# A kernel of four layers: every second weight of a 16-entry table is picked out by GpSimd, where it had every fourth

## The reference

```
layer 1  attention, 16 heads of 128 over 1024 rows (no mask), float32
layer 2  silu(x @ tern(W_up)) * (x @ tern(W_gate)) @ tern(W_down), tern(W) = clip(round(W / mean|W|)) * mean|W|
layer 3  causal attention over a latent of 64, 16 heads

def _ghost_linear(x, idx, lut):            # layer 4
    w = lut[idx]                           # lut has 16 float32 entries
    return jnp.einsum('bsh,oh->bso', x, w)
gate = _ghost_linear(x, gate_idx, lut)     # gate_idx, up_idx: 688 x 256 int32, 0..15
up   = _ghost_linear(x, up_idx, lut)
h    = jax.nn.silu(gate) * up
return _ghost_linear(h, down_idx, lut)     # down_idx: 256 x 688
```

## Time and profile before

| what | value |
|---|---|
| time, median of 3 runs | 882.39 us (881.47 to 882.75) |
| time of the profiled execution | 882.52 us |
| its span (first to last instruction) | 880.7 us |
| busy: PE, DVE, ACT, POOL | 93%, 87%, 69%, 49% of the span |
| instructions | 13310 |

### The profile page before, as it was taken

The page is one execution under the profiler, slowest core; times in us unless marked ns, Lnnn a source line. Parts: engine busy times, 40 slices in busy tenths (PEclk is TensorE's granted clock), DMA queues, the critical chain, the costliest instruction groups (busy, mean ns, idle before and its releaser), DMA issues.

```text
span 880.7 us, 13310 instructions
## 1 busy us (share of the span) xinstructions
PE 815.8 (93%) x4386; PEld 474.4 (54%) x4386; DVE 770.5 (87%) x1726; ACT 604.2 (69%) x1044; POOL 430.1 (49%) x459
## 2 busy tenths in 40 slices
PE   7889989999999989998998999989988999998997
PEld 3445544455455445454445454567755566564687
DVE  4888999999999999999999999856789898986646
ACT  5777767776778676776766776765765777768632
POOL 3334454444454448678769776125333454544300
PEclk8999999999999999999999999999989999999999
DMA  3588859957788668776875676821000000000001
GB/s 105 123 180 157 151 113 173 194 113 153 166 166 155 127 130 151 148 143 117 161 149 111 124 142 130 155 79 46 1 1 1 1 1 1 1 1 2 1 1 49
DMA packets 276869, 86.32 MB, mean 98 GB/s; under 512 B 267584, under 2 KB 272448, under 8 KB 276416
## 3 DMA queue, kind: packets, MB, share of 16 engines
q1 hardware_dynamic: 275520, 80.05, 47.0%
q0 software_dynamic: 992, 5.34, 2.2%
q10 hardware_dynamic: 288, 0.07, 0.0%
HBM read 17.29 MB, written 1.05 MB: 21 GB/s over the span
## 4 chain that ended last, share of the span: by engine, by line
DVE 41%; PE 38%; issue 9%; ACT 6%; DMA 3%; POOL 2%; DVEq 0%; SPq 0%; ACTq 0%; POOLq 0%
DVE EP L1689 11%; DVE ps L1674 10%; PE ps L1012 6%; PE ps L1014 5%; PE ps L1013 5%; PE ps L1035 4%; DVE ptm L1790 4%; PE ps L1246 3%; PE ps L1050 3%; PE ps L1281 3%; PE ps L1267 3%; DMA ET<-EP 2%; DVE OL L1750 2%; DVE ps L1873 2%; DVE rinv L1684 1%
## 5 line engine op out<-in xcount | busy, mean ns | idle before, releaser
L1445 ACT ACTIVATE EP<-ps,rinv 128x1024 f16<-128x1024 f32 x128 | 142.5, 1113 | 47.5 <-DVE rinv L1684 45.4
L1435 ACT ACTIVATE ps<-ps,nmax 128x1024 f32<-128x1024 f32 x128 | 139.3, 1088 | 49.2 <-DVE nmax L1674 42.8
L1674 DVE CUSTOM_DVE_ANT_0 ps<-ps,zero,q_unit 128x1024 f32<-128x1024 f32 x128 | 163.6, 1278 | 1.6 <-PE ps L1014 1.6
L1689 DVE SCALAR_TENSOR_TENSOR EP<-ps,rinv,EP 128x1024 f16<-128x1024 f32 x128 | 163.4, 1277 | 0.8 <-ACT EP L1445 0.5
L2039 POOL TENSOR_TENSOR wgu<-wgu,ptm 128x688 f32<-128x688 f32 x60 | 99.1, 1651 | 45.3 <-DVE ptm L1790 43.4
L1012 PE MATMUL ps<-ET,VH 128*128 128x512 f16 x256 | 97.0, 379 | 9.5 <-DMA ET<-EP 5.0
L1012 PE MATMUL ps<-K,Q 128*128 128x512 f16 x256 | 97.5, 381 | 8.7 <-DVE KR L1654 4.5
L2039 POOL TENSOR_TENSOR wdn<-wdn,ptm 128x512 f32<-128x512 f32 x45 | 57.2, 1272 | 93.2 <-DVE ptm L1790 92.1
L1014 PE MATMUL ps<-K,QR 128*128 128x512 f16 x256 | 97.0, 379 | 0.0
L1013 PE MATMUL ps<-KR,Q 128*128 128x512 f16 x256 | 97.0, 379 | 0.0
L1014 PE MATMUL ps<-ET,VL 128*128 128x512 f16 x256 | 97.0, 379 | 0.0
(11 more groups left out here) (256 smaller groups left out, 2119.3 us busy)
## 6 DMA issues: line engine op xcount, KB each, us to landing
wqr<-in_wqk SPq DMA_DIRECT2D x16, 256.0 KB, 3.6
wgu<-in_tern POOLq DMA_DIRECT2D x3, 1024.0 KB, 6.6
wvr<-in_wv SPq DMA_DIRECT2D x8, 256.0 KB, 4.1
wor<-in_wo SPq DMA_DIRECT2D x16, 128.0 KB, 3.1
ET<-EP SPq DMA_TRANSPOSE x128, 4.3
X<-in_x SPq DMA_DIRECT2D x2, 512.0 KB, 5.7
prw<-in_down_idx POOLq DMA_DIRECT2D x2, 256.0 KB, 5.1
tern<-in_l_wuq_rep SPq DMA_DIRECT2D x1, 512.0 KB, 4.1
```

The lines of the kernel that those rows point to most:

```text
L1435: e.activation(bank, bank, ACT.Exp, bias=nmax[:, c:c + 1], scale=-1.0, accum_out=rsum[:, c:c + 1]).then_inc(exped.sem, 1)
L1445: e.mul(EP[:, n % NE_RING, 0, :], SB(u, j), rinv[:, c:c + 1]).then_inc(e_hi.sem, 1)
L1674: e.tensor_tensor_reduce(SB(u, j), SB(u, j), zero[:, :].broadcast_to([P, 1024]), UNIT(h), 3.0e38, ALU.add, ALU.min, nmax[:, c:c + 1]).then ...
L1689: e.scalar_tensor_tensor(out=EP[:, n % NE_RING, 1, :], in0=SB(u, j), scalar=rinv[:, c:c + 1], in1=EP[:, n % NE_RING, 0, :], op0=ALU.mult, ...
```

## The change

The rule that says which picks GpSimd does goes from `v % 4 == 3` to `v % 2 == 1`. In each table GpSimd now makes the picks v = 1, 3, 5, ... 15 (eight, where it had four), and DVE makes v = 2, 4, ... 14 and v = 0. Half 1 of `ptm` is now written and read by GpSimd alone, and half 0 is written by DVE and read by GpSimd. Since DVE no longer makes pick 1, the add of v = 1 waits for DVE's v = 0 by a wait of its own (`picked[t, 0]`). Nothing else moves: the list of steps is the same.

```diff
-                (picked_g if v % 4 == 3 else picked).mark(t, v)
+                (picked_g if v % 2 == 1 else picked).mark(t, v)
...
-                    if v % 4 == 3:
+                    if v % 2 == 1:
                         continue
...
-                        if v % 4 == 3:
+                        if v % 2 == 1:
                             w.wait_ge(*index_in[t % 2][t])
                             w.wait_ge(*lut_in[0])
                             w.each([SUMS[step]])
                             e.tensor_scalar(ptm[:, 1, 0:n], index_tile(t), float(v), lut[:, v:v + 1], ALU.is_equal,
                                             ALU.mult).then_inc(picked_g.sem, 1)
-                        w.wait_ge(*(picked_g if v % 4 == 3 else picked)[t, v])
+                        w.wait_ge(*(picked_g if v % 2 == 1 else picked)[t, v])
                         if v > 1:
                             w.wait_ge(*lut_added[t, v - 1])
+                        else:
+                            w.wait_ge(*picked[t, 0])
                         e.tensor_tensor(dst, dst, ptm[:, v % 2, 0:n], ALU.add).then_inc(lut_added.sem, 1)
```

## The result

The changed kernel is slower: 886.27 us (median of 4 runs, 884.84 to 886.55) against 881.93 us (880.85 to 882.75), a ratio of 1.0041 with an interval of 1.0025 to 1.0057, that is 3.6 us. (The ratios in this document are those on record. They are not the quotients of the medians, which can differ by 0.1%: here 1.0049, or 4.3 us.) The forecast was 877.8 us and a range of 872.5 to 885.0. What came is nearest to the first rival, GpSimd's lateness on the path, some 2 us larger than it was priced. But 2.9 of the 3.7 us between the two profiled spans stand in two falls of TensorE's granted clock, which no rival had.

The account below looks back on a forecast made before the run. DVE was taken to set the pace in the 688-column tables, with PE and DVE taking turns before. The sum was 882.5 - 2.1 (small tables) - 3.5 (large tables) + 1.0 (`wol` wait) = 877.9, forecast 877.8 us, range 872.5 to 885.0.

Parts of the forecast that it names:

- the first rival: Tables of 688 columns: GpSimd's lateness reaches the path at `out_proj` and table 6, 3.8 us; 884.1 us in all, chance 0.19.
- GpSimd's busy sum: From 330 to 550 us, sixteen added picks bring GpSimd to 209 of 220 us busy, 95%, without the joints.
- The walk through GpSimd's new order: From 403.42 us in layer 1, GpSimd's steps followed one by one: `wol` ready at 421.6 instead of 417.7, 3.9 us late.
- PE stands still 0.9 us: PE waits for `wol` in `out_proj`, three times in the 688-column tables: 2.7 us if nothing hides it, 1 us charged.
- the 1.1 us at table 6: DVE's v = 0 of table 6 waits once for GpSimd's last add of table 5, about 1.1 us.
- I take half of the 7.0: Layer 1's 688-column tables: a gain of 3.5 us (bounds 0 and 7), as GpSimd also waits for others.
- The relief: 28 picks leave DVE, 19.6 us of work: 5.9 in the 512-column tables, 13.7 in those of 688.
- The picks' share of the chain: Path share of DVE's pick time: 35% at 512 columns, worth 2.1 us; 69% at 688, worth 9.5.
- The 7.0 of scarce engines: Three stretches from 337 to 545 us: layer 1 shortens by at most the scarcest engine's spare, 1.6 + 3.2 + 2.2 us.
- The port: DVE and GpSimd picks disturbing each other: taken as nil, 4 us either side; as third rival 21 us, 899 us, chance 0.03.

Follow-up runs that it names:

- large tables alone: The kernel before with the new pick rule only in tables 3 to 6 (688 columns): 886.95 us, ratio 1.0039 to before.
- relief alone: The changed kernel with GpSimd's new picks cut to two columns, except the first of tables 0 and 3: 876.68 us, 0.9922 of before.
- own index tile: The changed kernel with the odd tables' indices in a separate tile, so table 6 need not wait for table 5's last add: 887.21 us, 1.0048 of before.
- either edit alone: The changed kernel with only a separate tile for the odd tables' indices (887.21 us), or only the second split of `wo` moved earlier (887.52 us).
- edits alone: The kernel before, old pick rule, with a separate tile for the odd tables' indices and the second `wo` split earlier: 884.92 us, 1.0019 of before.
- early `wol`: The changed kernel with the second split of `wo` ahead of the splits of `wqk`: 887.52 us, 1.0051 of before.
- both edits: The changed kernel with a separate tile for the odd tables' indices and the second `wo` split earlier: 882.96 us, 1.0 of before.

## Why the prediction was wrong, step by step

**GpSimd's busy sum: right.** 209 us of 220 forecast, 208.19 measured. Its idle time before the adds of the large tables, 45.3 us in the earlier trace rows, of which 43.4 for DVE's picks, fell to 6.7, of which 1.9 for them (under 15 forecast).

**The walk through GpSimd's new order: right.** From the end of `q_unit` I had `wol` ready 18.2 us later. This is the stretch that answers to the earlier trace rows:

```profile
402.10 2.60 POOL L2034 TENSOR_SCALAR ptm<-prw,lut 128x688 f32<-128x688 int32 x1
404.78 3.42 POOL L2041 TENSOR_TENSOR wgu<-wgu,ptm 128x688 f32<-128x688 f32 x2
...
412.71 1.15 POOL L1993 TENSOR_TENSOR wql<-wqr,wqh 128x512 f16<-128x512 f32 x1
...
415.55 2.58 POOL L2034 TENSOR_SCALAR ptm<-prw,lut 128x688 f32<-128x688 int32 x1
418.21 1.64 POOL L2041 TENSOR_TENSOR wgu<-wgu,ptm 128x688 f32<-128x688 f32 x1
419.82 0.72 POOL L2015 TENSOR_TENSOR wol<-wor,woh 128x256 fp32r<-128x256 f32 x1
```

`wol` ends at 420.54, 18.4 us behind the start of the pick at 402.10. PE's wait there is 0.92 us, as forecast.

**"PE stands still 0.9 us", three times, of which I charged 1 us: too small.** I put the walk against PE as it ran before. PE gains a lead from DVE's relief, and then it waits for the lead as well: 1.60, 0.92 and 1.93 us, 4.4 in all. The same error is in the 1.1 us at table 6: DVE came 3.6 us earlier and waited 3.3.

**"I take half of the 7.0": this is the step that failed.** It was a gain of 3.5 us in the large tables. The large tables alone measure +3.4 us. The spare time of an engine is an upper bound for the gain when the engine never waits and nobody needs its results at a given time. GpSimd's results are needed at given times (`wol` once in four units, the last add of table 5), and there the others waited for it, 0.9 to 3.3 us each time. I had named these places, summed them at 3.8 us, and made them a rival at 0.19 with the right sign: 884.1 us, 1.7 over before, where 3.6 over before was measured (0.41%). Its number is nearer than its account: in the traces the kernel is 0.8 us behind at the 31st unit, and the clock adds the rest.

**The relief: over-sized in the large tables.** The picks' share of the chain gave 9.5 + 2.1 = 11.6 us, and the relief alone measured 6.9. The 7.0 of scarce engines was for GpSimd; with GpSimd free, PE has 32% of the chain, which is the likely reason why DVE's share of the chain before did not come through in full. (The prediction also calls the chain ahead of 330 us half PE; the lines shown have 38.2%.) In the small tables 2.1 us was forecast and 3.2 (1.8 to 4.6) measured.

**The port: right in the sum for the picks, for an incomplete reason, and it missed another instruction.** The 28 DVE picks left at 688 columns take 23.8 us, 0.28 us each above the undisturbed 0.57, which is what the 44 lost before. That the first and last parts of a GpSimd pick do hold a DVE pick up was not seen (last section). The prediction looked at picks alone. In table 4 and again in table 5 a GpSimd add now stands beside DVE's `vs` (L1732, a part of scaling the weights). Before:

```profile
391.74 0.29 DVE L1732 TENSOR_SCALAR vs<-vp 128x256 int32<-128x256 int32 x1
397.02 0.39 PE L1012 MATMUL ps<-ET,VH 128*128 128x512 f16 x1 [0.77 <-DVE VL L1663]
```

and in the changed kernel:

```profile
387.01 3.57 POOL L2041 TENSOR_TENSOR wgu<-wgu,ptm 128x688 f32<-128x688 f32 x2
388.98 1.75 DVE L1732 TENSOR_SCALAR vs<-vp 128x256 int32<-128x256 int32 x1
395.73 0.39 PE L1012 MATMUL ps<-ET,VH 128*128 128x512 f16 x1 [2.00 <-DVE VL L1663]
```

`vs` takes 1.46 us more and ends 0.15 us behind the adds. `VL` stands behind it in DVE's stream, and PE's wait for `VL` is 1.23 us longer. At 460 us it is the same, with a wait of 2.83. In the five kernels with eight picks in the large tables and DVE relieved, two of the eight `vs` take 1.74 or 1.75 us; in the other eight all take 0.29 or 0.30. The stretch from the 22nd to the 23rd unit's first L1689, which has the first of these places, is 20.20 us before and 1.5 to 1.8 longer in the five, and at most 0.4 longer in the others. No run takes this alone away, so what it costs at the end isn't shown.

**What I hadn't got: the clock.** It was put at nothing, without a reason. In the traces the stretches of low clock near 548 and 610 us stand for 1.67 and 1.2 us, 2.9 of the 3.7 between the spans, in parts that take the kernel with the large tables alone as long as the kernel before (13.56 and 322.3 us). The executions bear it out: the mean clock is 0.983 to 0.986 in the four of the changed kernel, and 0.988 to 0.994 in those of the kernel before that ran beside the experiments. Beside the run with its own index tile the kernel before took 880.36 to 882.10 us in its five executions at 0.992 or 0.993, and 882.45 to 885.00 in the twenty at 0.990 or below. What the falls near 397 and 493 us cost isn't settled (last section).

**What stays open:** how much of the 3.6 us of the medians is the clock's, since the 2.9 are read from one trace of each; how much of the loss is the held `vs`; why either edit alone gains nothing, beyond that DVE's waits for `ptm` grew when `wol` was moved and that both leave the held `vs`; the 1.7 us of the edits alone; and the lost gain when GpSimd takes all the picks of the small tables.

## What to carry to other kernels

Spare time as a share says little about an engine whose results others wait for at given places. Walk its new order from one such place to the next, and set it against the other engines where they will be after the gain, not where they were: a lead that you give to one engine comes back as its wait for the other. When a helper is moved to the idle engine, look for the stage in which that engine is the busiest, and split by stage: here the same rule is worth 0.4% in the small tables and costs as much in the large ones. Two waits in one chain may have to be removed together before either is seen to be worth something. Look in the trace also for instructions of other kinds that the moved work now lies beside (here `vs`), and at the granted clock: a wait of 2.3 us of TensorE was followed here by a stretch at half clock that cost 1.7 more.

The lowest kernel of this case has the new rule in the small tables alone, 0.9964 of before; six picks in the large tables on top of it (0.9971) are level with it within the intervals.

## What the runs showed of the hardware

**TensorE's granted clock fell to the lower level behind single waits of PE of 1.3 to 2.3 us, and this change made these waits longer.** Rows by stretch of the changed kernel (columns as in the earlier trace rows):

```profile
393.00:397.00 4.00, 1.77 (x9) 0.61 (x7) 3.93 (x9) 3.44 (x7) 3.77 (x3) 1.00 0.69 131
397.00:402.00 5.00, 4.98 (x17) 2.18 (x18) 3.53 (x7) 1.80 (x2) 4.72 (x6) 0.66 0.56 107
488.00:493.00 5.00, 3.07 (x19) 2.15 (x17) 4.83 (x9) 4.08 (x6) 4.92 (x4) 0.97 0.58 111
493.00:498.00 5.00, 5.00 (x19) 2.10 (x18) 1.62 (x5) 0.74 (x4) 4.62 (x3) 0.69 0.76 144
```

PE was busy 1.77 of 4 us, with the wait of 2.00 us for `VL` in it, and in the next 5 us the mean clock was 0.66, that is the level of 1.2 GHz for two thirds of them. At 488 PE had waited 1.93 us for `wol`, and 0.69 followed. Two more such stretches lie near 548 (behind a wait of 2.34 us for DVE's `EP`, 1.72 before) and 610 us (behind one of 1.30 us for `XL`, 1.12 before). The kernel before has none between 330 and 640 us. Each takes (1 - 0.66) x 5 = 1.7 us of full clock, 6.8 in all, which is the bound if PE were on the path throughout. The one near 548 us cost all of its 1.7 us (the 31st unit, above). The one at 610 us lies in a part where the kernels don't differ, and that part is 1.2 us longer. The one near 493 us cost nothing that shows: from the 28th to the 29th unit the kernel with the large tables alone, which has no fall there, loses 4.4 us and the changed one 4.3, both with the wait at table 6 in it. A fall did not follow every wait: with the large tables alone PE waited 2.35 us for `EP` near 550 us, and the clock stayed at 1.00; at 463.8 us of the changed kernel PE waited 2.83 us for DVE's `VL` and the clock stayed at 1.00 from 465 to 475, while the kernels with the large tables alone, with their own index tile and with the early `wol` show 0.66 from 470 to 475 behind the same wait, and the kernel with both edits shows 1.00 again. What decides it these runs don't tell.

**A GpSimd pick holds a DVE pick up at its two ends and not in its middle.** Timeline of GpSimd in the changed kernel:

```profile
384.34 2.59 POOL L2034 TENSOR_SCALAR ptm<-prw,lut 128x688 f32<-128x688 int32 x1
392.06 2.58 POOL L2034 TENSOR_SCALAR ptm<-prw,lut 128x688 f32<-128x688 int32 x1
...
415.55 2.58 POOL L2034 TENSOR_SCALAR ptm<-prw,lut 128x688 f32<-128x688 int32 x1
```

and of DVE, one pick in each of the three:

```profile
386.08 1.22 DVE L1790 TENSOR_SCALAR ptm<-prw,lut 128x688 f32<-128x688 int32 x1
393.05 0.57 DVE L1790 TENSOR_SCALAR ptm<-prw,lut 128x688 f32<-128x688 int32 x1
...
415.60 1.15 DVE L1790 TENSOR_SCALAR ptm<-prw,lut 128x688 f32<-128x688 int32 x1
```

The pick of 386.08 came 0.85 us before the end of GpSimd's, and ended 0.37 us behind it: it waited for the end. That of 393.05 came 1.0 us after the start and was not held. That of 415.60 came at the start and lost 0.58 us. These are three of many: in the changed kernel all eleven DVE picks of 688 columns that began 0.88 to 1.76 us into a GpSimd pick took 0.56 or 0.57 us, and all four that began with 0.53 to 0.85 us of it left ended 0.37 to 0.39 us behind it. The rule of the Trainium skill (SBUF — State Buffer, "Who interferes with whom"), that of GpSimd and a DVE instruction in a two-port mode whichever comes first has the shared pair for the whole instruction, fits GpSimd's adds and splits here (a DVE pick that met one with more than 0.2 us left ended 0.36 to 0.38 us behind it); for its pick the trace shows a middle of some 0.9 us in which a DVE pick can begin and isn't held.
